# Coattention: two of the output product's three sources as three float16 products each

## The reference

```
s    = xn @ diag(w_cq) @ y.T + (xn @ w_c) + (y @ w_q) + biases      # 256 x 77
a    = softmax(s, over the context);  c2q = a @ y                   # 256 x 256
b    = softmax(max of s over the context, over the tokens)          # 256
q2c  = b @ xn                                                       # 256
x   += [xn, c2q, xn*c2q, xn*q2c] @ W_l.T + b_l                      # 256 x 256
```

## Time and profile before

| | us |
|---|---|
| median of 3 runs (2645.31 to 2673.6) | 2656.15 |
| the profiled execution, its own time | 2657.47 |
| its span | 2655.8 |
| PE busy | 2191.8 (83%) |
| DVE busy | 1637.7 (62%) |
| ACT busy | 1190.9 (45%) |
| POOL busy | 1057.1 (40%) |
| the coattention stage in it | about 1604 to 1799 |

### The profile page before, as it was taken

How to read it: one execution, slowest core, us unless ns; L and a number is a source line. 1 busy time by engine, 2 the same in 40 slices (tenths; PEclk the granted TensorE clock), 3 DMA queues, 4 the chain that set the end, 5 groups by cost and what they waited for, 6 DMA issues and landing times. The chain is left out here.

```text
span 2655.8 us, 46285 instructions
## 1 busy us (share of the span) xinstructions
PE 2191.8 (83%) x16966; PEld 1564.2 (59%) x16966; DVE 1637.7 (62%) x3322; ACT 1190.9 (45%) x1892; POOL 1057.1 (40%) x1203
## 2 busy tenths in 40 slices
PE   7588888887677729993899997995299999999996
PEld 6355555554455617872566666885167676767674
DVE  4578777785788665651777764555655555555552
ACT  1344445553211216651555553323264647474742
POOL 3976677660000012313555411210244545454533
PEclk9799999998887759996999997996599999999998
DMA  4000000000000113321001100003143434343422
GB/s 205 1 1 1 0 0 0 0 0 1 9 6 5 64 66 121 124 92 42 25 24 27 21 1 15 15 10 126 57 109 97 99 97 99 97 99 97 99 66 32
DMA packets 62560, 135.92 MB, mean 51 GB/s; under 512 B 10688, under 2 KB 46736, under 8 KB 55568
## 3 DMA queue, kind: packets, MB, share of 16 engines
q0 software_dynamic: 30976, 52.45, 9.7%
q1 hardware_dynamic: 31504, 82.41, 8.9%
HBM read 100.22 MB, written 34.60 MB: 51 GB/s over the span
## 5 line engine op out<-in xcount | busy, mean ns | idle before, releaser
L2957 ACT ACTIVATE f_h<-bank,f_b 128x512 f32<-128x512 f32 x256 | 175.9, 687 | 280.5 <-PE bank L176 273.3
L176 PE MATMUL ring<-f_w2hi,f_hidhi 128*128 128x256 f16 x1024 | 280.0, 273 | 6.0 <-DVE f_hidlo L2994 3.7
L2994 DVE TENSOR_TENSOR f_hidlo<-f_h,f_hidhi 128x512 f16<-128x512 f32 x256 | 177.3, 692 | 173.2 <-ACT f_hidhi L2958 172.0
L176 PE MATMUL ring<-f_w2hi,f_hidlo 128*128 128x256 f16 x1024 | 279.9, 273 | 0.0
L176 PE MATMUL ring<-f_w2lo,f_hidhi 128*128 128x256 f16 x1024 | 279.8, 273 | 0.0
L3048 POOL DMA_INDIRECT out<-f_y,f_to_row x128 | 211.8, 1655 | 47.7 <-issue 34.1
L176 PE MATMUL bank<-f_xthi,f_w1hi 128*128 128x512 f16 x512 | 195.2, 381 | 4.9 <-DVE f_w1lo L2977 4.9
L176 PE MATMUL bank<-f_xtlo,f_w1hi 128*128 128x512 f16 x512 | 195.1, 381 | 0.0
L176 PE MATMUL bank<-f_xthi,f_w1lo 128*128 128x512 f16 x512 | 195.1, 381 | 0.0
L1755 POOL COPY c_from_row<-c_token 128x5 uint32 (+1 forms) x8 | 1.5, 184 | 435.0 <-POOLq L1482 356.3
L2958 ACT ACTIVATE f_hidhi<-bank,f_b 128x512 f16<-128x512 f32 x256 | 173.9, 679 | 0.0
(11 more groups left out here) (519 smaller groups left out, 6001.7 us busy)
## 6 DMA issues: line engine op xcount, KB each, us to landing
f_raw<-in_e_w SPq DMA_DIRECT2D x32, 1024.0 KB
c_raw<-in_e_w SPq DMA_DIRECT2D x16, 1024.0 KB, 6.0
slots_out<-c_y POOLq DMA_DIRECT2D x8, 640.0 KB, 3.7
x<-in_x SPq DMA_DIRECT2D x1, 4096.0 KB, 23.9
tokens<-c_xn SPq DMA_DIRECT2D x16, 256.0 KB, 2.3
out<-x SPq DMA_DIRECT2D x1, 4096.0 KB, 13.7
tokens<-f_xn SPq DMA_DIRECT2D x16, 256.0 KB, 2.2
wb<-in_wb SPq DMA_DIRECT2D x1, 3096.0 KB, 31.8
```

Of the source, the lines that this page charges most:

```text
L176: mm = pe.matmul(out, left[a], right[b], start=first and n == 0, stop=last and n == 2)
L2957: act.activation(h32[n % 4][:, :], src, ACT.Gelu_apprx_tanh, bias=bias).then_inc(sig["h_full"], 1)
L2994: dve.tensor_tensor(hid_v[1][:, it, at], h32[n % 4][:, :], hid_v[0][:, it, at], ALU.subtract).then_inc(sig["h_lo"], 1)
```

## The change

The products of `c2q` and of `cc` become three float16 products each; the third source stays float32. Each float32 operand is kept as a float16 high part and a float16 remainder. For the weights this is done once, before the first pair: ScalarE copies 128x1024 to float16, VectorE subtracts. For each pair ScalarE makes the high parts of `c2q` (from PSUM) and of `cc` (from SBUF), VectorE the remainder of `c2q` (`low_c2q`), GpSimd the remainder of `cc`. The product of source 0 waits for `cq_low_ready` and that of source 1 for `cc_low_ready`. On VectorE the two new subtractions stand behind the update with twin 0's product and ahead of `q2c`.

```diff
+        w_parts = [ctx.enter_context(nc.sbuf_tensor(f"e_w_{part}", [P, 2 * KT * D], F16)) for part in ("hi", "lo")]
...
@@ PE, product()
                     if t == 0 and k == 0:
-                        pe.wait_ge(u["c2q_ready"], i.now)
+                        pe.wait_ge(u["cq_low_ready"], i.now)
                         pe.wait_ge(u["x_updated"], i.before)
                     if t == 0 and k == 1:
-                        pe.wait_ge(u["cc_ready"], i.now)
+                        pe.wait_ge(u["cc_low_ready"], i.now)
...
                     for h in range(KT):
-                        left = (u.cq_v[q], u.cc_v[q], u.xt_v[q])[k][:, h, tok]
-                        right = (w_l[:, 1, h, :], w_l[:, 2, h, :], u.we_v[q][:, h, :])[k]
-                        mm = pe.matmul(u.out[:, t * D:(t + 1) * D], left, right, start=k == 0 and h == 0,
-                                       stop=k == 2 and h == KT - 1)
+                        out = u.out[:, t * D:(t + 1) * D]
+                        if k < 2:
+                            split_product(pe, out, [a[:, h, tok] for a in u.mid_v[q][k]],
+                                          [w[:, k, h, :] for w in w_split], k == 0 and h == 0, False)
+                        else:
+                            mm = pe.matmul(out, u.xt_v[q][:, h, tok], u.we_v[q][:, h, :], start=False,
+                                           stop=h == KT - 1)
...
@@ ACT, pair()
                         act.activation(u.c2q_t[q][:, :], u.c2q_out, ACT.Copy).then_inc(u["c2q_ready"], 1)
-
+                        act.activation(u.cq_parts[q][0][:, :], u.c2q_out, ACT.Copy).then_inc(u["cq_high_ready"], 1)
+                    for u in twins:
+                        act.wait_ge(u["cc_ready"], i.now)
+                        act.activation(u.cc_parts[q][0][:, :], u.cc_t[q][:, :], ACT.Copy).then_inc(u["cc_high_ready"], 1)
+
+                act.activation(w_parts[0][:, :], w_mid, ACT.Copy).then_inc(sig["w_high_made"], 1)
                 norm(0, Turn(0, None), 0)
...
@@ POOL, pair()
+                    for u in twins:
+                        pool.wait_ge(u["cc_high_ready"], i.now)
+                        pool.tensor_tensor(u.cc_parts[q][1][:, :], u.cc_t[q][:, :], u.cc_parts[q][0][:, :], ALU.subtract
+                                           ).then_inc(u["cc_low_ready"], 1)
...
@@ DVE
+                def low_c2q(u, q, i):
+                    dve.wait_ge(u["c2q_ready"], i.now)
+                    dve.wait_ge(u["cq_high_ready"], i.now)
+                    dve.tensor_tensor(u.cq_parts[q][1][:, :], u.c2q_t[q][:, :], u.cq_parts[q][0][:, :], ALU.subtract
+                                      ).then_inc(u["cq_low_ready"], 1)
...
                     if ago is not None:
                         update(twins[0], ago)
+                    for u in twins:
+                        low_c2q(u, q, i)
                     for u in twins:
                         dve.wait_ge(u["q2c_made"], i.now)
...
                 similar_weights(Turn(0, 1))
+                dve.wait_ge(sig["w_high_made"], 1)
+                dve.tensor_tensor(w_parts[1][:, :], w_mid, w_parts[0][:, :], ALU.subtract).then_inc(sig["w_low_made"], 1)
```

More of the change, by code:

```diff
@@ L2330, in coattention @@
         wq_v = tiles(w_q_wide[:, :], KT)
+        l_at = WB_AT["l"][0]
+        w_mid = mem.wb[:, l_at + KT * D:l_at + 3 * KT * D]
+        w_parts = [ctx.enter_context(nc.sbuf_tensor(f"e_w_{part}", [P, 2 * KT * D], F16)) for part in ("hi", "lo")]
+        w_split = [w[:, :].rearrange("p (k h o) -> p k h o", k=2, h=KT) for w in w_parts]
         twins = []
@@ L2344, in coattention @@
                                                       for n in ("xn", "xn_t", "c2q_t", "cc_t", "w_eff"))
+            u.cq_parts, u.cc_parts = ([[ctx.enter_context(nc.sbuf_tensor(f"e_{n}_{part}{p}{q}", [P, W2], F16))
+                                        for part in ("hi", "lo")] for q in range(2)] for n in ("cq", "cc"))
             u.c_v, u.sw_v = (tiles(t[:, :], KT) for t in (u.c_t, u.sim_w))
-            u.xt_v, u.cq_v, u.cc_v, u.we_v = ([tiles(t[:, :], KT) for t in both]
-                                              for both in (u.xn_t, u.c2q_t, u.cc_t, u.w_eff))
+            u.xt_v, u.we_v = ([tiles(t[:, :], KT) for t in both] for both in (u.xn_t, u.w_eff))
+            u.mid_v = [[[tiles(t[:, :], KT) for t in parts[q]] for parts in (u.cq_parts, u.cc_parts)] for q in range(2)]
             u.a_v = tiles(u.a[:, :])
@@ L2450, in _ @@
                 pe.wait_ge(sig["w_q_ready"], 1)
+                pe.wait_ge(sig["w_low_made"], 1)
                 last = in_parities(pe, pair)
```

## The result

The changed kernel took 2701.85 us (median of 4 runs, 2687.19 to 2704.19). The kernel before, in 4 runs, took 2664.88 (2645.31 to 2675.47). The ratio estimated from all these runs is 1.0121, with a 95% interval of 1.0077 to 1.0165 (the two medians alone would give 1.0139). The forecast was 2677 and within 1%, the range went to 2694, so the time lies above the range. The change makes the kernel slower, clear of noise.

What follows compares the result with a forecast made beforehand. PE is nearly full, but a wait on VectorE was taken to close each round. The profiled 2657.5 us plus 12.8 for longer waits less shorter calls, plus 7 for PE's clock, gave 2677; the range was 2656 to 2694.

Steps and rivals of the forecast that it cites:

- The call: PE's product: six float16 matmuls take 0.65 us instead of 0.86 for float32, saving 0.21 in 64 of 96 calls.
- The first part at full clock: Round from twin 1's transposes to ACT's copy of twin 0's `c2q`: 14.51 us before, 1.05 comes out, 13.46.
- The second part's chain: VectorE's work from ACT's `c2q` copy to twin 1's next transposes: 10.4 us instead of 7.3, +21.7 over seven rounds.
- PE's gap: PE idle in each round before twin 0's transposes, waiting for VectorE: 3.8 us.
- a collision of two SBUF-input instructions: VectorE's subtractions, 0.69 us each alone, wait for POOL's bias additions; the second ends at 9.05 after ACT's copy.
- The end of the stage: Shorter calls at the end: -1.05 for the last first part, -0.4 and -1.7 for later calls, together -3.2 us.
- Rival 4: VectorE's subtractions don't collide or slip between POOL's instructions: second part +1.4 to +1.9, 2658 to 2662 us; chance 0.13.
- rival 5: Faster: VectorE's subtractions run while it waits for twin 1's `e_c_t`, rounds shrink by 1.7 us: 2645 us; chance 0.07.
- the wait at the start: Before the first pair: ACT's copy of the weights' high part costs +1.0 us, VectorE's remainder of them is hidden.
- the clock: PE's clock falls after its idle time in the round, 1.2 us in each of six rounds: +7 us.
- rival 1: The terms as summed, with the clock falling in part of the rounds: 2677 us; chance 0.45.
- the sum of +19.8: All terms over the profiled 2657.5 us: +12.8 for waits and savings together, +7 for the clock.

Runs made afterwards that it cites:

- e3: Changed kernel, but POOL's bias additions wait until ACT has copied the transposed `xn`; stage 203.9 us against 222.8 in the changed kernel.
- e4: Changed kernel plus twelve unread transposes of `a` on PE ahead of its wait, in rounds between first and last pair; stage 213.8 us against 222.8.
- e1: Changed kernel without VectorE's remainders of `c2q`; PE multiplies by the high part twice instead, so the output lacks a term; stage 208.3 us against 222.8.
- e2: Changed kernel with the product of `cc` float32 again, without ACT's `cc` copies and POOL's remainders; stage 214.1 us against 222.8.
- e5: Changed kernel with PE's wait for the weights' remainder moved from the top of its program to its first product; stage 219.3 us against 222.8.

## Why the prediction was wrong

**Right, by its own steps.** The call: 0.65 us for six float16 products. The first part at full clock: 13.46 forecast, 13.46 in e3 and e4. The second part's chain, in the round shown: the remainders end at 8.8 us after ACT's copy (forecast 9.05), twin 0's transposes come at 9.1 (9.3), twin 1's at 10.2 (10.4); seven rounds +20.7 against +21.7. PE's gap 3.54 (3.8). The cause, a collision of two SBUF-input instructions in the chain that closes the round, is shown from three sides: without the remainders (e1), without POOL's remainders (e2), with the bias additions moved (e3). The end of the stage: -1.9 where -2.1 were due beside the last first part. Rival 4 (no collision) and rival 5 (faster) are refuted: `e_cq_lo` has a median of 1.6 us and the round is 25. POOL's late bias addition took 1.70 to 1.72 in place of 1.26: 0.45 more, between the 0.33 of the earlier trace rows and the 0.55 by the rule of the Trainium skill (SBUF — State Buffer, "SBUF: two separate sides"), so neither was exact.

**Failed: the wait at the start.** The prediction had "Their remainder on DVE is hidden: DVE waits there for the first similarity over 2 us" and put +1.0 for the start. ACT's copy did cost that 1.0. But the remainder was not asked after from the side of PE: its wait stands ahead of PE's loop, so the first transposes wait until VectorE has done `e_sim_w` and then `e_w_lo`. The start measured +4.65, 3.65 more than the sum had for it; e5, which moves only this wait, gave 3.7 back at the start and 3.5 in the stage.

**Mis-sized: the clock.** "I take 1.2 in six rounds: +7." The first parts exceed 13.46 by 1.16, 2.28, 1.30, 2.42, 1.37 and 2.46 in turn, 11.0 in all, 1.83 each. The mechanism is right (e4 gave 8.8 back in these parts without touching the waits). The fall came in every one of the six rounds, lasting for 3.4 and 6.8 us by turns and costing 1.3 and 2.4 on the mean, where rival 1 had it in part of the rounds and short. That is +4.0. The trace of before could have warned of it. The first attention has four gaps of PE of 3.04 us (from 231.5, 377.2, 448.3 and 521.5), and the prediction names one that brought a fall and one that didn't; the other two brought one as well, so it was three in four, and the falls lasted 3.4, 6.8 and 3.4 us.

**Mis-based: the range.** The stage's +26.6 us against one execution at 2657.5 gives 2684, inside the range; the sum of +19.8 was 6.8 short in the stage, from 3.7 for the wait and 4.0 for the clock less 1.0 in the second parts. The measured median stands 18 us higher still. 7.4 of this is the median of before, which is 2664.9 in four runs, 2660.7 in 17 and 2668.7 in 29. The other 10.4 the stage doesn't account for. The profiles point to the clock outside the stage: among the four runs of the changed kernel, the three at 2699.7 to 2704.2 had a mean granted clock of 0.897 to 0.900, and the one at 2687.2 had 0.905. In the later series of twelve, whose median was 2687.71, inside the range, that excess is gone. So the two failed steps alone would not have left the range; with the base they bring the time to 2691.5, its upper end. That the rest was chance, in which executions four runs caught, is likely and not shown. The sum has no term for either, though the prediction knew that runs of the kernel before lay 1% apart. A range of this kind has to be laid around what executions of the kernel before show, not around one profile. The chance for slower (0.27) went by 2683 as the line, 6 us above the forecast; each of the two failed steps pushed toward it, and whether it came to more than 1% the two series (1.0121 and 1.0092) leave open.

## What to carry to other kernels

An engine that is busy for 96% of a round may still be closed by another engine's queue, so ask first which wait ends each round, and put new work behind the read that releases it: the order on VectorE's queue alone moved this stage from +26.6 to -8.5 us, and a fuller reorder with PE's wait moved as well to -19.1. For each wait that a change adds, those ahead of a loop too, look up what the waiting engine does next and what is queued ahead of the signal. A gap opened on PE can be paid twice: here once as the gap of 3.54 us, and once in the clock behind it, 1.83 us a round.

## What the runs showed of the hardware

- GpSimd's float32 minus float16 to float16 over 512 columns takes 1.15 us undisturbed, less than a float32 product of two tiles of the same size (1.27).
- A VectorE instruction with two SBUF inputs that was ready during a GpSimd one took 1.3 to 1.75 us instead of 0.69, and the GpSimd instruction behind it 1.60 to 1.72 instead of 1.15 to 1.27; in the round shown they take turns, one each.
- PE's granted clock was 0.50 over 1786.80 to 1790.20, after PE had stood idle for 3.54 us. But in e3, with 1.74 us idle before the transposes, it fell in four of six rounds, and in e4, with 2.23 us idle but twelve more transposes ahead, it didn't in four of six. So the last gap's length doesn't decide it by itself.
- A stretch of another stage, with the same code, took 74.6 us in seven profiles and 87.0 in six; between the first two the whole difference is PE's busy time, 35.04 and 47.40 us, at a granted clock of 0.60 and 0.51.
